# Filter stage of a graph network kernel: gathers released by quads instead of by chunks

## The reference

```
filt = silu(rbf @ Wf1 + bf1) @ Wf2 + bf2      # per edge, rbf has 20 values
msg = x[col] * filt                           # per edge, 256 values
agg = segment_sum(msg, row, num_segments=N)   # per node
```

## Time and profile before

| | us |
|---|---|
| median of three runs | 5103.01 |
| profiled execution, its time | 5104.09 |
| profiled execution, its span | 5102.3 |
| filter stage, first gather to last store's landing and barrier | about 2698 to 3302 |

### The profile page before, as it was taken

One profiled execution on the slowest core, in us unless ns is written; L12 is line 12 of the kernel. 1 busy time (PEld: TensorE's weight loads), 2 busy tenths in 40 slices (PEclk: granted clock), 3 DMA queues, 4 the chain that ended last, 5 costly groups with the idle time before them and its releaser, 6 DMA issues. The chain is left out here.

```text
span 5102.3 us, 75134 instructions
## 1 busy us (share of the span) xinstructions
PE 3706.8 (73%) x20786; PEld 2965.0 (58%) x20786; DVE 2898.2 (57%) x5915; ACT 1658.3 (33%) x3757; POOL 2644.4 (52%) x2597
## 2 busy tenths in 40 slices
PE   7883539476898999813608999848999858777178
PEld 6662327365777777602406888726777646666065
DVE  8783528056787888743127898724333545554553
ACT  5562213101333333201205766523333313333033
POOL 0055645566777777557576777630000067776400
PEclk6586659788999999855759999977999967887579
DMA  5044444458999999723417888711000046776300
GB/s 75 9 161 145 120 142 140 145 182 268 294 307 299 300 309 302 229 79 94 128 48 203 244 242 238 212 51 59 0 0 0 23 135 192 198 199 190 110 13 25
DMA packets 642022, 779.41 MB, mean 153 GB/s; under 512 B 149190, under 2 KB 562361, under 8 KB 638106
## 3 DMA queue, kind: packets, MB, share of 16 engines
q0 software_dynamic: 120624, 316.61, 20.6%
q1 hardware_dynamic: 350852, 284.27, 19.8%
q10 hardware_dynamic: 170374, 176.38, 11.0%
HBM read 509.08 MB, written 272.20 MB: 153 GB/s over the span
## 5 line engine op out<-in xcount | busy, mean ns | idle before, releaser
L2018 POOL DMA_INDIRECT a_far<-kv_table,a_index x416 | 486.0, 1168 | 146.0 <-issue 118.3
L1447 POOL DMA_INDIRECT by_dst<-dst_row,place x416 | 415.4, 999 | 261.9 <-issue 121.0
L2599 POOL DMA_INDIRECT fl_far<-x_table,fl_index x416 | 453.3, 1090 | 143.9 <-issue 126.5
L2333 POOL DMA_INDIRECT a_far<-src_table,a_index x416 | 452.9, 1089 | 132.1 <-issue 123.1
L2636 PE MATMUL ps<-fl_w,fl_hid 128*128 128x256 f32 x1664 | 398.8, 382 | 20.1 <-ACT ps L2708 19.0
L2052 PE MATMUL ps<-a_w,a_edge_t 128*128 128x256 f32 x1664 | 407.1, 389 | 0.0
L3304 POOL DMA_INDIRECT starts<-p_near,p_at x25 | 24.3, 974 | 709.2 <-DMA starts<-p_zero 694.1
L2636 PEld LDWEIGHTS ps<-fl_w,fl_hid 128*128 128x128 f32 x1664 | 309.5, 191 | 66.4 <-issue 27.5
L2188 DVE TENSOR_TENSOR a_far<-ps,a_far 128x1024 f32<-128x1024 f32 x208 | 253.9, 1220 | 164.9 <-PE ps L2052 148.0
L2052 PEld LDWEIGHTS ps<-a_w,a_edge_t 128*128 128x128 f32 x1664 | 311.4, 197 | 36.1
L1078 ACT ACTIVATE f_hid<-ps,f_bn 128x320 f32<-128x320 f32 x320 | 197.6, 617 | 328.6 <-PE ps L1032 328.6
(11 more groups left out here) (535 smaller groups left out, 9476.9 us busy)
## 6 DMA issues: line engine op xcount, KB each, us to landing
partial<-a_out ACTq DMA_DIRECT2D x208, 546.0 KB, 4.6
a_edge<-by_dst SPq DMA_DIRECT2D x104, 516.0 KB, 6.4
partial_f<-fl_out ACTq DMA_DIRECT2D x26, 2056.0 KB
dst_row<-in_edge_attr SPq DMA_DIRECT2D x52, 1024.0 KB, 5.9
xn_sb<-q_table SPq DMA_DIRECT2D x416, 128.0 KB
fl_keys<-key_rows SPq DMA_DIRECT2D x26, 1024.0 KB, 5.3
a_keys<-local_rows SPq DMA_DIRECT2D x104, 128.0 KB
xt<-partial SPq DMA_DIRECT2D x14, 512.0 KB, 4.9
```

Source lines behind the costliest of these rows:

```text
L1447: self.nc.gpsimd.indirect_dma_start(out=self.table, out_offset=bass.IndirectOffsetOnAxis(ap=self.place[:, n:n + 1], axis=0), in_=self.row[ ...
L2018: gathered[b % 4].count(nc.gpsimd.indirect_dma_start(out=far[:, b, u, :], out_offset=None, in_=kv_table, in_offset=bass.IndirectOffsetOnAx ...
L2333: gathered[b].count(nc.gpsimd.indirect_dma_start(out=far[:, b, u, :], out_offset=None, in_=src_table, in_offset=bass.IndirectOffsetOnAxis( ...
L2599: gathered[q * 4 + t // 4].count(nc.gpsimd.indirect_dma_start(out=far[:, q, t, :], out_offset=None, in_=table, in_offset=bass.IndirectOffs ...
```

## The change

`chunk_free` is no longer waited for by GpSimd. A new semaphore `quad_taken` starts at 4 and is raised by VectorE once per quad, behind its wait for the second half's multiply and ahead of the cast L2818. GpSimd waits for it ahead of each quad's four gathers, for m + 1, so that quad m is issued when quad m - 4 has been multiplied. The wait for `indexed` stays ahead of a chunk's first quad. `pool_passed` is raised per quad instead of per chunk. SyncE still waits for `chunk_free`.

```diff
--- before.py
+++ after.py
@@ -2537,9 +2537,9 @@
         keys_loaded = [st.sem("keys_loaded0"), st.sem("keys_loaded1")]
         sp_passed = st.sem("sp_passed")
         names = ("chain", "weights_split", "indexed", "rbf_turned", "rbf_copied", "hid_ready", "hid_done", "keys_turned", "keys_kept", "keys_written", "filtered", "same_made",
-                 "bias_laid", "opened", "msg_ready", "high_made", "low_made", "summed", "copied", "chunk_free", "pool_passed")
+                 "bias_laid", "opened", "msg_ready", "high_made", "low_made", "summed", "copied", "chunk_free", "pool_passed", "quad_taken")
         (chain, weights_split, indexed, rbf_turned, rbf_copied, hid_ready, hid_done, keys_turned, keys_kept, keys_written, filtered, same_made,
-         bias_laid, opened, msg_ready, high_made, low_made, summed, copied, chunk_free, pool_passed) = map(st.sem, names)
+         bias_laid, opened, msg_ready, high_made, low_made, summed, copied, chunk_free, pool_passed, quad_taken) = map(st.sem, names)
         RBF, HIDB, KEYS, FILT, SUMS = 0, (1, 2), 3, (4, 5), (6, 7)
         PAIRS = CHUNKS // 2
         QUADS = CHUNKS * 4
@@ -2588,15 +2588,15 @@
             @block.gpsimd
             def _(pool):
                 with pool.Fori(0, CHUNKS // 2) as i:
-                    for q in range(2):
-                        c = i * 2 + q
-
-                        pool.wait_ge(indexed, c + 1)
-                        pool.wait_ge(chunk_free, c + 1)
-
+                    for qb in range(8):
+                        q, b = qb // 4, qb % 4
+                        if b == 0:
+                            pool.wait_ge(indexed, i * 2 + q + 1)
+
+                        pool.wait_ge(quad_taken, i * 8 + qb + 1)
                         pool.sem_inc(pool_passed, 1)
-                        for t in range(CT):
-                            gathered[q * 4 + t // 4].count(nc.gpsimd.indirect_dma_start(out=far[:, q, t, :], out_offset=None, in_=table,
+                        for t in range(b * 4, b * 4 + 4):
+                            gathered[qb].count(nc.gpsimd.indirect_dma_start(out=far[:, q, t, :], out_offset=None, in_=table,
                                                          in_offset=bass.IndirectOffsetOnAxis(ap=index[:, q, t:t + 1], axis=0),
                                                          bounds_check=NPAD - 1, oob_is_err=False))
 
@@ -2771,6 +2771,7 @@
                 ch = Chain(dve, chain)
                 dve.wait_ge(loaded, 112)
                 dve.sem_inc(chunk_free, 2)
+                dve.sem_inc(quad_taken, 4)
                 ch.link(nc.vector.tensor_scalar(low_part[:], core.c("iota_p"), float(2 * NG), None, ALU.is_ge))
                 raw, to, low = w1_raw, w1_sb, low_part[0:NG4, 0:1]
                 ch.link(nc.vector.tensor_copy(to[:], raw[:]))
@@ -2815,6 +2816,8 @@
                                                     far[:, q, at:at + 2, :], ALU.mult).then_inc(msg_ready, 1)
 
                             dve.wait_ge(msg_ready, m * 2 + v + 1)
+                            if v == 1:
+                                dve.sem_inc(quad_taken, 1)
                             nc.vector.tensor_copy(msg_high[:, to, :], msg[:, to, :]).then_inc(high_made, 1)
                             dve.wait_ge(high_made, m * 2 + v + 1)
                             nc.vector.tensor_tensor(msg_low[:, to, :], msg[:, to, :], msg_high[:, to, :], ALU.subtract).then_inc(low_made, 1)
```

## The result

The changed kernel took 5082.62 us in the median of nine runs (5070.78 to 5094.29), the kernel before 5100.69 (5089.7 to 5126.44) beside it: ratio 0.996, interval 0.9941 to 0.9979. 5106 was forecast. Later, on four chips on which the same kernel takes over 5700 us, the change turned out to be worth 2.6 to 3.8%; that is the larger part of what follows.

The account below looks back on a forecast made before the run. GpSimd's gather stream was taken to pace the filter stage, with VectorE full between stalls. Increments +2.9 and a semaphore clear +0.07 gave +3.0 us, 5106.0 against the median of 5103.01; range 5098 to 5120.

Parts of the forecast that it names:

- GpSimd's clockwork isn't moved: Filter stage: GpSimd's gather stream keeps its pace, so VectorE's lateness is taken up whenever it waits for a gather.
- increment's path: VectorE, ahead of the cast: only the increments of quads 75 to 103 stay on the path, 29 x 0.1 = 2.9 us.
- rival E: Filter stage: faster, as waits for the keys' broadcast go; at most -3.4 us by the last gather's landing, 5099.6; chance 0.08.
- rival B: GpSimd's gathers: held behind the multiply, each quad's first starts beside VectorE's cast and lengthens; +61 us, 5164; chance 0.01.
- No row has GpSimd held: GpSimd's release by quads: the new wait delays no gather, 1.8 us being left even at quad 93; cost 0.
- it can only hold: GpSimd's release by quads: the new rule is never earlier than the old, so it can't start any gather sooner.
- Increment 0.1 us each: VectorE, between the second multiply's wait and the cast L2818: each of 104 increments costs 0.1 us.
- Semaphore clear, +0.07: End of the filter stage: one more semaphore to clear, +0.07 us.
- What bounds the stage: the stream: Filter stage: GpSimd's unbroken gather stream, 1.394 us each, paces it on average; between stalls VectorE is full.
- Rival A: Third quads of a chunk: held gathers land too late and VectorE stalls; +38.6 us, 5142; chance 0.05.
- Range: Whole kernel: 5098 to 5120 us, taking in E, D, the forecast and C up to 0.16 us per increment.

Follow-up runs that it names:

- lead 8: The changed kernel with quad_taken starting at 8 instead of 4; ratio to the kernel before 0.999 on chip 5, 0.9987 on chip 1.
- half_rows: The kernel before with each gather fetching 512 bytes a row instead of 1024, from other rows; ratio 1.0005 on chip 5.

## Why the prediction was wrong

- **"GpSimd's clockwork isn't moved" (increment's path; rival E).** This is the step that failed. I had the stage's pace from it, 1.394 us a gather, and took it as given for the kernel after. The pace was 1.374 there (570.4 / 415). The forecast's terms of +2.9 and +0.07 stand beside a term that I had set at nothing and that measured -8.3 us in the profiled pair. The pace moves from trace to trace: the five other traces on chips of the first kind, that of after among them, have streams of 568.0 to 584.6 us beside the 578.7 of before. With one trace for each kernel it can't be said how much of that is the kernel's and how much the execution's. Rival E's bound, -3.4 us, rested on the same step and so gave a range that ended too high. The maximum of 1589 ns was in the earlier trace rows, and rival B used it, but for a rise alone. The term doesn't close the account: 5106 less 8.3 is 5097.8, and 5082.62 was measured. The other 15 us are in no profile, and their cause stays open.
- **Rival B and its page.** The Trainium skill's page SBUF — State Buffer, section A bandwidth-pool intuition that's wrong, has a VectorE copy that keeps GpSimd from writing descriptors until it ends. The traces agree: a gather that starts 0.05 to 0.1 us into the cast takes 1.21 to 1.23 us, and it ends 0.87 us behind the cast's end. They add that a subtraction with two SBUF operands does the same, and for longer, as it lasts 0.69 us and not 0.43. So the rival had the mechanism; it looked at it for held gathers alone, and not for those that fall on such an instruction anyway.
- **"No row has GpSimd held" as a ground for cost 0 (the hold).** Right on the chip of the trace: the new wait holds no gather, and the least margin is 5.37 us. But I took from "it can only hold" that it can't gain. Where GpSimd isn't the pacer the hold gains 155 to 212 us, since there a long run of gathers goes with stalls of the others that GpSimd's own stream doesn't show. One profile of one chip had no row of it; that a profile might be another chip's wasn't among my cases.
- **Increment 0.1 us each.** Right: 0.11. The Trainium skill's page VectorE: DVE Perf Modes, section The DRAIN you can't avoid, by which a semaphore behind each copy costs nothing extra, again doesn't fit an increment that is an instruction of its own. The +2.9 us that I put on the path isn't seen: from the last gather's start to the last store are 13.3 us before and 13.4 after. In lead 8 it is 15.8, so this end varies by as much as the term. All 104 on the path would be 1.0023 on that chip; the two runs of the increments alone gave 1.0006 and 1.0015, on chips where VectorE mostly waits, so they don't say how much is on the path where it doesn't.
- **Semaphore clear, +0.07.** Below what these runs can tell.
- **What bounds the stage: the stream.** Right on the first kind of chip: stage less stream is 35.1 to 39.7 us in all six traces. Wrong elsewhere: 52.1 us in the unchanged kernel on chip 3, where the stream itself holds 369.6 us more idle time than before's.
- **Rival A.** Not reached at a limit of 4: the landings that ended a wait in after took 7.6 to 8.0 us, where 12.7 would have been needed. Its mechanism shows at 3 (20 waits for gathers, ratio 1.0028).
- **Range.** Chances of 0.91 for no change that can be measured went with a range whose lower end was 5 us below the median. The measured ratio, 0.996, lies within the 0.5% of "same"; the time lies outside the range since the stream's own spread had no term in it.

## What to carry to other kernels

A stream of gathers issued by GpSimd has no fixed pace: give it a term with both signs, from the spread of its instructions' durations and from what VectorE runs when they start. A limit on how far it runs ahead can be free on one chip and worth 2.6 to 3.8% on another. Start from the least that covers the landing, by the rows of the kernel at hand (here four quads; three cost 0.3% on the one chip where they were tried), and time such a change on several chips before it is judged.

## What was not expected of the hardware

- **Two kinds of chips, or of occasions.** The same kernel takes 5090 to 5101 us on two occasions and 5705 to 5789 us on four others. On chip 3 the dense stages are equal to the first chip's (560.8 and 560.8, 190.7 and 190.7 us), and the four stages with 208 gathers or more are longer: 971.6 for 614.0, 1126.8 for 1031.7, 724.0 for 614.6, 382.7 for 328.9.
- **TensorE's completions come late beside gathers there**: 5.4 and 7.9 us behind the matmul's end in one burst and 0.03 us in the pause behind it, while VectorE's and ScalarE's semaphores rise within 0.01 us of their ends.
- **A gather ends 0.86 to 0.88 us behind the end of the VectorE instruction in which it started**, if that instruction reads SBUF alone, had begun at least 0.045 us before and had over 0.25 us to run; this makes gathers of 1.2 to 1.6 us out of those of 1.0.
- **Half the bytes, the same time**: `half_rows` moves 189 GB/s in the stage where before moves 235, with gathers of 1.010 us in the median and a stage of 614.2 us.
